# One GpSimd instruction for the drives of two states, a lead of four slots, and an earlier second chunk, in a selective-scan and feed-forward block

## The reference

```python
h = layernorm(x) * (1 + ca) + sa
x = x + ga * ssm(h)                  # selective scan
h = layernorm(x) * (1 + cb) + sb
x = x + gb * ffn(h)                  # silu(g) * u, then down

# ssm(x): dt, B, C = split(x @ x_proj_w.T);  delta = softplus(dt @ dt_proj_w.T + b)
#   for each token t:  h = exp(delta_t * A) * h + delta_t * B_t * x_t     # (256, 16)
#                      y_t = sum_n h[:, n] * C_t[n] + D * x_t
```

## Time and profile before

| | |
|---|---|
| time, median of 3 runs | 325.35 us (325.25 to 325.63) |
| the profiled execution | 325.3 us, with a span of 323.4 us between its first and last instruction |
| busy, share of the span | PE 257.2 us (80%), DVE 258.4 (80%), POOL 226.9 (70%), ACT 184.1 (57%) |
| granted TensorE clock, mean | 0.841 |
| 63 drives on GpSimd | 147.7 us |
| 29 products on GpSimd | 68.5 us |
| 128 half scans on DVE | 157.4 us (119.6 + 37.8) |

### The profile page before, as it was taken

The page is one execution under the profiler, slowest core; times in us unless marked ns, Lnnn a source line. Parts: engine busy times, 40 slices in busy tenths (PEclk is TensorE's granted clock), DMA queues, the critical chain, the costliest instruction groups (busy, mean ns, idle before and its releaser), DMA issues. The chain is left out here.

```text
span 323.4 us, 3838 instructions
## 1 busy us (share of the span) xinstructions
PE 257.2 (80%) x1231; PEld 192.4 (60%) x1231; DVE 258.4 (80%) x365; ACT 184.1 (57%) x294; POOL 226.9 (70%) x113
## 2 busy tenths in 40 slices
PE   7884999727366985965999998839897986888995
PEld 7652996415254653743857676628685864665874
DVE  3599569999568899979999999699989996952320
ACT  2687547765154885896258947932364795141400
POOL 1008969999997999799569996996499999000000
PEclk9985569985557899875699999776999795999999
DMA  7849617594264445392425733725536600001002
GB/s 249 310 99 166 146 56 221 107 224 135 72 87 70 98 106 98 78 145 40 130 68 73 162 100 101 151 41 158 104 98 142 120 0 0 0 2 65 2 0 69
DMA packets 33173, 33.09 MB, mean 102 GB/s; under 512 B 14912, under 2 KB 20224, under 8 KB 33152
## 3 DMA queue, kind: packets, MB, share of 16 engines
q1 hardware_dynamic: 32736, 32.01, 44.0%
q10 hardware_dynamic: 416, 0.81, 0.8%
HBM read 30.40 MB, written 2.36 MB: 101 GB/s over the span
## 5 line engine op out<-in xcount | busy, mean ns | idle before, releaser
L624 POOL TENSOR_TENSOR drv<-u,brow 128x1024 f32<-128x1024 f32 x63 | 147.7, 2366 | 18.3 <-DVE u L899 16.7
L977 DVE TENSOR_TENSOR_SCAN state<-decay,last,drv 128x512 f32<-128x512 f32 x96 | 119.6, 1269 | 14.2 <-ACT decay L812 13.9
L812 ACT ACTIVATE decay<-delta,A 128x512 f32<-128x512 f32 x128 | 87.4, 687 | 75.8 <-DVE state L977 74.4
L1293 PE MATMUL sums<-ident,drv 128*128 128x128 f32 x512 | 76.9, 306 | 5.0 <-POOL drv L636 4.6
L1293 PEld LDWEIGHTS sums<-ident,drv 128*128 128x128 f32 x512 | 67.0, 158 | 17.3 <-issue 8.8
L636 POOL TENSOR_TENSOR drv<-state,crow 128x1024 f32<-128x1024 f32 x29 | 68.5, 2362 | 11.2 <-DVE state L977 11.1
L952 DVE TENSOR_TENSOR drv<-state,rows_ps 128x512 f32<-128x512 f32 x70 | 46.3, 662 | 9.1 <-PE rows_ps L1267 9.1
L1267 PE MATMUL rows_ps<-c_parts,sel 64*128 64x512 f32 x35 | 21.0, 599 | 37.4 <-DVE drv L952 37.4
L977 DVE TENSOR_TENSOR_SCAN state<-decay,drv 128x512 f32<-128x512 f32 x32 | 37.8, 1208 | 0.1
L1214 PE MATMUL side<-h_hi,ffn_hi 128*128 128x512 f32 x76 | 31.6, 502 | 6.2 <-DVE gates L924 5.2
L1267 PEld LDWEIGHTS rows_ps<-c_parts,sel 64*128 64x128 f32 x35 | 7.7, 219 | 47.5 <-DVE drv L952 38.0
(11 more groups left out here) (142 smaller groups left out, 299.9 us busy)
## 6 DMA issues: line engine op xcount, KB each, us to landing
brow<-bc_dram SPq DMA_DIRECT2D x31, 512.0 KB, 5.6
crow<-bc_dram SPq DMA_DIRECT2D x13, 512.0 KB, 6.5
resid<-in_x SPq DMA_DIRECT2D x4, 512.0 KB, 5.1
out<-resid SPq DMA_DIRECT2D x8, 256.0 KB, 2.2
gates<-in_wmod ACTq DMA_DIRECT2D x1, 768.0 KB, 6.1
gates<-in_wmod SPq DMA_DIRECT2D x1, 768.0 KB, 7.9
last<-state SPq DMA_DIRECT2D x48, 1.0 KB, 2.2
crow<-bc_dram SPq DMA_DIRECT2D x3, 256.0 KB, 4.6
```

The source lines that it names most:

```text
L624: nc.gpsimd.tensor_tensor(drv[j % RING_DRV][:, :, 0:S], u[:, c % 2, :, 0:S], b.unsqueeze(1).to_broadcast([P, HALVES, S]), ALU.mult).then_i ...
L812: nc.scalar.activation(decay[i % RING_DECAY][:, 0:S], delta[:, c % 2, h, 0:S], ACT.Exp, scale=A[:, h * N + n:h * N + n + 1]).then_inc(deca ...
L977: nc.vector.tensor_tensor_scan(state[j % RING_STATE][:, h, 0:S], decay[i % RING_DECAY][:, 0:S], drv[j % RING_DRV][:, h, 0:S], before, ALU. ...
L1293: ins = nc.tensor.matmul(sums[:, b * D + h * P:b * D + (h + 1) * P], of[:, h, b * P:(b + 1) * P], ident[:, :], is_transpose=True, start=Fa ...
```

## The change

Two states' drives become one instruction of 128x2048, `LEAD` becomes 4, and the preparation of chunk 1 is moved one slot ahead, except its `st0`, `st1` and `agg`, which have an entry of their own. The 12 drive buffers become one tile, so that two neighbours can be written at once; `drive` is called for even n only, and the semaphore `drive_ready` now counts groups. The first call makes 0.1 alone (0.0 is still DVE's).

```diff
-LEAD = 3
+LEAD = 4
...
-            for later in (0, SECOND_LATER.get(name, 2)) if kind == "F" and plan is PLAN else (0,):
+            for later in (0, SECOND_LATER.get(name, 1)) if kind == "F" and plan is PLAN else (0,):
...
-        drv = [sb(f"drv{i}", [P, HALVES, MAXC]) for i in range(RING_DRV)]
+        drives = sb("drives", [P, RING_DRV, HALVES, MAXC])
+        drv = [drives[:, i, :, :] for i in range(RING_DRV)]
...
         def upto_drive(c, n):
-            return c * N + n
+            return (c * N + n) // GROUP + 1
...
-                    sp.wait_ge(drive_ready, GROUP * (group - RING_B + 1) - 1)
+                    sp.wait_ge(drive_ready, group - RING_B + 1)
...
             def drive(c, n):
 
                 S, j = CHUNK[c], c * N + n
-                if n == (c == 0):
+                first, group = 1 if j == 0 else 0, j // GROUP
+                if n == 0:
                     pool.wait_ge(*u_made(c))
-                if n % GROUP == 0 or j == 1:
-                    group = j // GROUP
-                    pool.wait_ge(brow_loaded[group % RING_B], 16 * (group // RING_B + 1))
-                if j in [to for to, _ in EQUAL]:
+                pool.wait_ge(brow_loaded[group % RING_B], 16 * (group // RING_B + 1))
+                if any(j <= to < j + GROUP for to, _ in EQUAL):
 
                     pool.wait_ge(same_ready, len(EQUAL))
                 if j >= RING_DRV:
 
-                    pool.wait_ge(added, j - RING_DRV + 1)
-                b = brow[(j // GROUP) % RING_B][:, n % GROUP, 0:S]
-                nc.gpsimd.tensor_tensor(drv[j % RING_DRV][:, :, 0:S], u[:, c % 2, :, 0:S],
-                                        b.unsqueeze(1).to_broadcast([P, HALVES, S]),
-                                        ALU.mult).then_inc(drive_ready, 1)
+                    pool.wait_ge(added, j + GROUP - RING_DRV)
+                size, at = [P, GROUP - first, HALVES, S], j % RING_DRV
+                b = brow[group % RING_B][:, first:, 0:S]
+                nc.gpsimd.tensor_tensor(drives[:, at + first:at + GROUP, :, 0:S],
+                                        u[:, c % 2, :, 0:S].unsqueeze(1).to_broadcast(size),
+                                        b.unsqueeze(2).to_broadcast(size), ALU.mult).then_inc(drive_ready, 1)
...
                     if step == 0 and slot == 0:
-                        for n in range(1, LEAD):
+                        for n in range(0, LEAD, GROUP):
                             drive(0, n)
                     for task in side_tasks("gpsimd", step, slot):
                         side_work(*task)
                     if step >= 0:
                         for c, n in lagged(step, slot, -LEAD):
-                            drive(c, n)
+                            if n % GROUP == 0:
+                                drive(c, n)
```

## The result

The changed kernel takes 334.09 us (median of 4 runs, 332.66 to 334.67), the kernel before 325.49 in its 4 runs beside it. The ratio is 1.025, with a 95% interval of 1.0207 to 1.0293: slower by some 8.6 us, where 8.5 were forecast. The profiled execution took 333.6 us with a span of 331.8.

A forecast was written before the change was run, and what follows sets the result against it. GpSimd is full in step 0 and sets its end through `nmr_F`; later DVE sets the pace. The profiled 325.3 us plus 8.5, with nothing added afterwards, gave 333.8 us; main range 331.8 to 336, whole range 329.6 to 336.8.

The forecast's parts named there:

- The first wait: Start of step 0: ACT's `xn0` waits for `nmr_F` ahead of the decay of 0.1, half 1; scan at 33.2, +4.1 us.
- `S wb` and `xT`: Step 0, PE: `xT` of chunk 1 now precedes `S wb`, adding 0.9 us; DVE's row 2 product at 47.95, +5.0.
- The landings and pairs on GpSimd: Step 0: groups 5 and 6 land at 55.6 and 63.4, then 33.3 us of work; `nmr_F` of chunk 2 at 96.7, +8.5.
- DVE's waits for products: Late step 0: scan 0.13 waits 2.8 us for its buffer, scan 0.15 1.9 more; steps towards the same 8.5.
- the moves of `hmod`, `z`, ... I cost at nothing: Chunk 1 preparation on ACT, PE and DVE, one slot sooner: no cost, since each engine has its inputs there.
- The gate: Second half of scan 1.0, which ends step 0: at 98.6 in place of 90.10, +8.5 us.
- Afterwards: Steps 1 to 3, behind 98.6: every DVE time keeps its +8.5; further cost nothing (0 to +1.5 us).
- No new waits of DVE behind that: Trace sign: no new DVE waits after the second half of scan 1.0 at 98.6; last scan some 8.5 us later.
- The pair's price: GpSimd: one 128x2048 pair costs 4.45 us (4.2 to 4.7) against 4.64 for two drives; 31 pairs save about 6 us.
- The queue order alone: Rival: the first wait weighs nothing on DVE, `nmr_F` of chunk 2 at 91.7; +3.5, 328.8 us, chance 0.06.
- the ACT wait: Rival: the ACT wait in step 0 is the only loss, GpSimd's later products stay covered; +5.0, 330.3 us, chance 0.13.
- The saving of the merge is handed on: Rival: eight pairs ahead of `nmr_F` of chunk 2 save 0.19 each, 1.5 us; 323.8 us, chance 0.04.

The follow-up runs named there:

- Experiment 3: The changed kernel with `nmr_F` of chunk 1 put ahead of all drives in GpSimd's queue; 328.74 us, ratio 1.011.
- experiment 1: The changed kernel with chunk 1's preparation back at two slots later, except `nmr` (as changed) and `u` (slot 12); 330.09 us, ratio 1.0128.
- Experiment 6: Experiment 3's kernel with the B rows of groups 2 to 7 of each chunk planned one slot sooner; 325.93 us, ratio 1.0019.
- experiment 7: Experiment 3's kernel with GpSimd's product placed before its pair in each slot; 330.2 us, ratio 1.0148.
- experiment 5: The changed kernel, pairs kept, with `LEAD` back at 3 and chunk 1's preparation as in the kernel before; 324.56 us, ratio 0.9967.
- experiment 10: The kernel before, single drives, with only `nmr_F` of chunk 2 moved directly behind `u` of chunk 1 on GpSimd; 320.25 us, ratio 0.9841.
- experiment 4: The changed kernel with each pair made by two 128x1024 instructions in the same order, the merge undone; 334.32 us, ratio 1.0272.

## Why the prediction was right, step by step

- *The first wait.* Forecast +4.1 on the scan of 0.1, half 1, from `nmr_F` at 31.2 to 31.4. Found: `nmr_F` at 31.70 and the scan +4.6 with a first scan that began 0.5 later, thus +4.1. Experiment 3 removes exactly this by removing its cause, and experiment 1 by putting `xn0` back behind the decay.
- *`S wb` and `xT`.* Forecast `S wb` from 37.6 and row 2's product +5.0. Found: 37.98 and +5.2 (+4.7 from the first scan).
- *The landings and pairs on GpSimd.* Forecast waits for rows until 55.6 and 63.4, then 33.3 us without a gap to 96.7. Found: 55.80, 63.36, 96.74; the two transfers took 5.1 and 6.3 us, where 5.1 and 6.6 were taken over from before. Experiment 6 shows what the landings are worth once the first wait is gone (2.8 us in time), experiment 7 that the products themselves were not the limit.
- *DVE's waits for products.* Forecast 2.8 at scan 0.13 and 1.9 at scan 0.15. Found: 0.74 at 0.13 and 1.88 at 0.15. For the 0.74 the profile names a decay, but the decay that this scan needs had ended at 79.84, and the product of 0.9 at 80.77; scan 0.13 came at 80.97, as long after that product as scan 0.15 after its own. The wait is short because DVE had lost 1.9 us already behind `z`. So the step "the moves of `hmod`, `z`, ... I cost at nothing" was wrong: they delay DVE by 1.9 us at scan 0.6. That this does not show in the sum is luck: GpSimd's queue set the end of the step, and the lost time lay within its waits.
- *The gate.* Forecast 98.6; found 98.68, of which 0.5 is the later first scan. From the first scan it is +8.1 where +8.5 were forecast, so the agreement to a tenth is partly chance. *Afterwards* forecast 0 to +1.5; found -0.7 (from +8.6 to +7.9 in the two profiles), and as far as the medians tell (+8.6), nothing. "No new waits of DVE behind that" was not quite so: there are two, 1.0 us together, made up for by shorter waits for PE.
- *The pair's price.* Forecast 4.45, found 4.49 from start to start. For all drives 6 us of GpSimd's work were to be saved; found 4.6 (147.7 us busy before, 143.1 after). The Trainium skill, "GPSIMD Engine Reference", Elementwise — side-by-side cycle accounting, gives 4497 ns for a `tensor_tensor` add of 2048 float32 columns. The trace agrees, for a multiply: the pairs are busy 4.50 to 4.60 us, and the next instruction starts 4.49 later.
- *The rivals.* Each names a part of the loss, and neither is the whole. The queue order alone costs 4.8 us (experiment 1), more than the 3.5 worked out for it; the ACT wait, taken away in experiment 3, gives back 5.3. Together that is more than the loss. At the gate the parts do add up: 3.7 us in experiment 1, close to the 3.5, and 4.0 taken back in experiment 3, 7.7 of 8.1. The excess lies behind the gate, where the distance grows by 0.5 us in the profile of experiment 1 and shrinks by 1.6 in that of 3. The saving of the merge is handed on only in experiment 5, 1.0 us, where the lead and the preparation are those of the kernel before.
- *The range.* Its ends do not follow from its terms. The ACT wait alone is 330.3 by the rival's own sum, and 329.6 in the range; pairs, landings and the later steps at their upper values give 337.3 and not 336. The measured 334.09 lies within either.

## What to carry to other kernels

Moving a task sooner in one queue moves it in front of other work; it gains nothing unless its input comes sooner too, and here it put a waiting instruction of 1 us in front of the decay that the scan needed. Before moving work forward on a full engine, ask which small instructions queue behind it and who waits for those: 0.15 us saved a pair stood against one more pair, 4.5 us, ahead of a 0.2 us `nmr_F`. The merge itself did no harm; at a lead of three it gained 1.0 us. Ask too whether the inputs of the work moved forward come in time: with the B rows a slot sooner, and the first `nmr_F` out of the way, the loss was gone. And look in the kernel before for the wait that such a small instruction already causes: moving it, with nothing else changed, gave 5.0 us (experiment 10).

## What the runs showed that was not expected

The first scan began at 25.0 to 27.0 us in the profiles, at 25.0 and 26.7 in two kernels that are the same up to there, so a difference of 1 to 2 us between two single profiles can come from the loads at the start. The medians moved less than that: the kernel before had 325.3, 325.6 and 325.3 in the three sets of runs, but its single runs lay between 323.2 and 327.2. An effect like that of the merge alone (experiment 4, +0.2 in the medians, 1.0 in the profile) is not to be told from the time of four runs; in experiment 5 it took twelve.
